# A block-placed copy of the values: GpSimd products with a mask column in the place of DMA copies

## What is computed

```python
xa = layer_norm(x)
w, k, v, r, g = projections(xa, shifted(xa))      # w is a decay between 0 and 1
def step(s, rkvw):                                # one token, per head, s is 16 x 16
    a = k_t[..., :, None] * v_t[..., None, :]
    out = einsum('bhi,bhij->bhj', r_t, u * a + s)
    s = a + w_t[..., :, None] * s
    return s, out
out = group_norm(scan(step, s0, (r, k, v, w))) * silu(g)
x1 = x + out @ Wo.T
x2 = x1 + sigmoid(xr2 @ Wfr.T) * (relu(xk2 @ Wfk.T) ** 2 @ Wfv.T)
```

## Time and profile before

| | |
|---|---|
| median of 3 runs | 3357.83 us (3356.09 to 3358.71) |
| the profiled execution | 3359.69 us, its span 3358.0 us |
| TensorE matmuls, weight loads | busy 95%, 71% |
| VectorE, ScalarE, GpSimd | busy 78%, 56%, 7% |
| mean granted TensorE clock | 0.987 of full speed |
| L1921 issues on GpSimd | 192, 528 ns mean |
| L489 issues on SP | 192, 64 KB each, median 1.9 us to landing |

### The profile page before, as it was taken

How to read it: one execution, slowest core, us unless ns; L and a number is a source line. 1 busy time by engine, 2 the same in 40 slices (tenths; PEclk the granted TensorE clock), 3 DMA queues, 4 the chain that set the end, 5 groups by cost and what they waited for, 6 DMA issues and landing times.

```text
span 3358.0 us, 77396 instructions
## 1 busy us (share of the span) xinstructions
PE 3205.9 (95%) x33056; PEld 2390.2 (71%) x33056; DVE 2628.4 (78%) x3721; ACT 1884.6 (56%) x3113; POOL 226.0 (7%) x457
## 2 busy tenths in 40 slices
PE   6889999999999999999999999998999999998998
PEld 4667777777777777777777777776566666665666
DVE  2888888989888888888888898987447567566566
ACT  2556555565565555555555555554346656556555
POOL 0000000000000000000000000000101010010110
PEclk8889999999999999999999999999999999999999
DMA  3113322333333223333332233324324234133221
GB/s 117 60 70 114 114 101 98 121 139 106 110 114 114 103 97 123 121 117 114 114 114 101 98 119 125 103 106 159 107 57 116 51 75 111 32 89 103 62 68 48
DMA packets 91924, 336.82 MB, mean 100 GB/s; under 512 B 16704, under 2 KB 37824, under 8 KB 65600
## 3 DMA queue, kind: packets, MB, share of 16 engines
q0 software_dynamic: 39936, 234.91, 21.6%
q1 hardware_dynamic: 51216, 93.68, 8.7%
q10 hardware_dynamic: 432, 3.28, 0.2%
HBM read 252.11 MB, written 16.78 MB: 80 GB/s over the span
## 4 chain that ended last, share of the span: by engine, by line
PE 73%; DVE 21%; ACT 3%; issue 1%; DMA 1%; SPq 0%; DVEq 0%; ACTq 0%
PE psum L729 31%; DVE rw L1647 6%; PE psum L738 6%; PE psum L904 5%; PE psum L922 3%; DVE rw L1630 3%; PE psum L874 3%; PE psum L864 3%; PE psum L779 3%; PE psum L894 3%; DVE rw L1529 2%; DVE psum L1737 2%; PE psum L879 2%; DVE rw L1535 2%; PE psum L682 2%; PE psum L803 1%
## 5 line engine op out<-in xcount | busy, mean ns | idle before, releaser
L729 PE MATMUL psum<-rw 128*128 128x256 f32 x6144 | 1412.7, 385 | 10.3 <-DVE rw L1535 4.9
L729 PEld LDWEIGHTS psum<-rw 128*128 128x128 f32 x6144 | 1150.8, 191 | 214.1 <-issue 42.6
L1647 DVE TENSOR_TENSOR rw<-rw 128x2048 f32<-128x2048 f32 x192 | 432.8, 2286 | 33.4 <-PE psum L803 30.3
L1737 DVE CUSTOM_DVE_ANT_0 psum<-psum,mem 128x1024 f32<-128x1024 f32 x256 | 313.4, 1224 | 81.1 <-PE psum L894 80.9
L1286 ACT ACTIVATE rest<-psum,mem 128x1024 f32<-128x1024 f32 x256 | 284.9, 1113 | 80.1 <-DVE mem L1737 78.4
L1195 ACT ACTIVATE rw<-psum 128x512 f32<-128x512 f32 x192 | 199.3, 1150 | 128.8 <-PE psum L779 128.8
L904 PE MATMUL psum<-ident,rest 128*128 128x128 f32 x2048 | 269.4, 275 | 0.2 <-ACT mem L1279 0.2
L904 PEld LDWEIGHTS psum<-ident,rest 128*128 128x128 f32 x2048 | 235.0, 141 | 38.5 <-issue 13.1
L1529 DVE SCALAR_TENSOR_TENSOR rw<-psum,rw 128x256 f32<-128x256 f32 x480 | 196.1, 475 | 83.4 <-PE psum L695 43.5
L1921 POOL DMA_DIRECT2D rw<-big_dram x192 | 101.2, 528 | 2309.6 <-PE psum L729 2275.7
L894 PE MATMUL psum<-side 128*128 128x512 f32 x512 | 211.8, 495 | 23.0 <-ACT rest L1286 20.7
(11 more groups left out here) (153 smaller groups left out, 4421.3 us busy)
## 6 DMA issues: line engine op xcount, KB each, us to landing
rw<-big_dram POOLq DMA_DIRECT2D x192, 1024.0 KB, 5.2
side<-mem POOLq DMA_DIRECT2D x256, 128.0 KB, 4.3
rw<-xs_dram SPq DMA_DIRECT2D x32, 512.0 KB, 3.5
side<-mem SPq DMA_DIRECT2D x256, 64.0 KB, 2.1
rw<-rw SPq DMA_DIRECT2D x192, 64.0 KB, 1.9
xs_dram<-rw SPq DMA_DIRECT2D x24, 512.0 KB, 5.3
rw<-x_dram SPq DMA_DIRECT2D x16, 512.0 KB, 3.6
mem<-xs_dram SPq DMA_DIRECT2D x16, 512.0 KB, 4.4
```

The lines of the kernel that those rows point to most:

```text
L729: last = mm(t[:, o * TC:(o + 1) * TC], big[:, k, P * m:P * m + P], src[:, k, 0:TC], start=k == 0, stop=k == KT - 1, skip_group_check=True)
L1647: state_dve.inc(tt(s_bd[:, half, :, :].rearrange("p c (h j) -> p c h j", h=4), own, place, ALU.mult), it, f"b{k}{half}")
L1737: maxima.inc(nc.vector.tensor_tensor_reduce(t, t, mbias.rearrange("p (a s) -> p a s", a=2), 1.0, 3.4e38, ALU.add, ALU.min, accum_out=mx[:, ...
```

## The change

`v_m` is filled by GpSimd: for each unit and pair four `tensor_scalar` products, each over all 128 partitions and 512 columns, of `v_t` with one column of a mask `place`, which is 1 on the partitions of chunk c and 0 elsewhere. VectorE makes the mask at the start. The clear of `v_m` and SP's copies go. GpSimd's weight loads, before one loop over the list, are now written in TensorE's order, and the products stand between them. The waits of the products are those that the copies had. The first weight loads now stand behind the wait for the constants.

```diff
+        place = sb("place", [P, 4])
...
-        vm_loaded = sem("vm_loaded")
+        chunks = Steps(sem("chunks"), ["m0", "m1"])
...
             for s in range(ITS + 2):
                 e, c, b, n = s - 2, s - 1, s, s + 1
-                if b < ITS:
-                    load_vm(b, 0)
                 if 1 <= n < ITS - 1:
                     load_xl(n + 1)
-                if b < ITS:
-                    load_vm(b, 1)
...
                 if n == 0:
-                    pe.wait_ge(vm_loaded, 16 * 4 * (2 * it + pair + 1))
+                    pe.wait_ge(chunks.sem, chunks.at(it, f"m{pair}"))
...
-            cleared(part_of("v_m"))
...
-            dve.wait_ge(const_ready, 9)
+            nc.vector.tensor_reduce(place[:], ident[:].rearrange("p (m c) -> p c m", c=4), AX_X, ALU.add).then_inc(const_ready, 1)
+            dve.wait_ge(const_ready, 10)
...
-            for turn, (it, which) in enumerate(weights):
-                if turn >= NSLOT:
-                    old_it, old = weights[turn - NSLOT]
-                    tiles, name = last_tile[old]
-                    pool.wait_ge(tiles.full, tiles.full_at(old_it, name))
+            pool.wait_ge(const_ready, CONSTS)
+
+            def fetch(turn):
+                it, which = weights[turn]
                 nc.gpsimd.dma_start(part_of(f"slot{turn % NSLOT}"), a["big"][layer_of(it), which]).then_inc(slot_loaded[turn % NSLOT], 16)
 
+            def after(it, which):
+                tiles, name = last_tile[which]
+                pool.wait_ge(tiles.full, tiles.full_at(it, name))
+                if turn_of[it, which] + NSLOT < len(weights):
+                    fetch(turn_of[it, which] + NSLOT)
+
+            def by_chunk(it, pair):
+                if pair == 0:
+                    pool.wait_ge(*b_ring.empty_at(it, "VT1"))
+                    if it:
+                        pool.wait_ge(b_ring.full, b_ring.full_at(it - 1, "U13"))
+                else:
+                    pool.wait_ge(b_ring.full, b_ring.full_at(it, "U03"))
+                for c in range(4):
+                    last = nc.gpsimd.tensor_scalar(v_m[:, :, c, :], v_t[:, :, 256 * pair:256 * pair + 256], place[:, c:c + 1], None, ALU.mult)
+                chunks.inc(last, it, f"m{pair}")
+
+            for turn in range(NSLOT):
+                fetch(turn)
+            for s in range(-1, ITS + 2):
+                e, c, b, n = s - 2, s - 1, s, s + 1
+                has_e, has_c, has_b, has_n = 0 <= e < ITS, 0 <= c < ITS, 0 <= b < ITS, n < ITS
+                if has_e:
+                    after(e, WFR)
+                if has_b:
+                    by_chunk(b, 0)
+                if has_c:
+                    after(c, WO)
+                if has_e:
+                    after(e, WFK)
+                if has_b:
+                    by_chunk(b, 1)
+                if has_e:
+                    after(e, WFV)
+                if has_n:
+                    after(n, WV)
+                    after(n, WK)
+                    after(n, WR)
+                    after(n, WG)
```

More of the change, by code:

```diff
@@ L133 @@
 OUT_PE = ["b00", "b01", "b10", "b20", "b21", "b30"]
-CONSTS = 10
+CONSTS = 11
 def laid_out():
@@ L477, in store_x @@
                 sp.dma_start(a["xs"][half_of(it), batch_of(it)], x1_flat[it % 2]).then_inc(x_stored, 16)
[L479 to L489, removed]
             def load_context(b):
@@ L1162, in spread_queries @@
                 if it == 0:
-                    act.wait_ge(zeroed, 3)
+                    act.wait_ge(zeroed, 2)
                 else:
```

## The result

The changed kernel takes 3624.46 us (median of 4 runs, 3622.98 to 3633.61), beside 3358.27 for the kernel before (4 runs). The ratio is 1.0786, with a 95% interval of 1.0765 to 1.0807: 7.9% slower. The profiled execution took 3624.39 us, its span is 3622.3, 264.3 more than before. The prediction said 3363, with a range of 3352 to 3400.

The account below looks back on a forecast made before the run. The prediction took TensorE, almost never idle in the units between 220 and 900 us, as the bound. 5.5 + 3.2 - 3.8 = +4.9 us on the profiled 3359.7 gave 3364.6, so 3363 for the median, range 3352 to 3400.

Parts of the forecast that it names:

- What bounds the kernel, and where the products must fit: Units at 220 to 900 us: TensorE busy 676.8 of 680.0; room 11.1 us for pair 0, 8.1 for pair 1.
- the first rival: Pair 1's last products let in late around VectorE's run: 3374 to 3384, some 3420 with the clock down; chance 0.30.
- The price of one product: GpSimd's 128x512 product: 0.65 us, between 0.52 and 1.08; four make 2.6 us.
- Does it disturb VectorE?: Both pairs: the products' full 2.6 us charged as a delay of VectorE, absorbed by its own slack.
- The wait of L662 for L1484: Pair 0: TensorE waits 0.25 us for late VectorE in each of 22 units, 5.5 us.
- Both signs: Prediction wrong if a product costs over 0.8 us, or the clock falls below 1.00 between 220 and 2300 us.
- The other edits: SP's issues, GpSimd's weight-load order, later first loads, v_m's clear, mask column: together nothing.
- What is gained: Unit of 1462 us: the 2.08 us copy wait and L729's slower matmuls behind it go, 3.8 us together.
- The 2.08 us at 1462: TensorE's wait for SP's copies in a middle unit, 2.08 us, expected gone.
- The sum: Whole kernel: 5.5 for pair 0, 3.2 for units 0 and 1, less 3.8 gained: +4.9 us.

Follow-up runs that it names:

- e4: Changed kernel with 12 memsets of 128x512 in place of each four products: 3375.70 us, ratio 1.0039 to the kernel before.
- e7: Changed kernel with e1's edit, and VectorE waiting for pair 1's products ahead of its run: 3509.39 us, ratio 1.0439 to the kernel before.
- e3: Changed kernel with products over 256 of the 512 columns, the other half of v_m left zero: 3402.17 us, ratio 1.0119 to the kernel before.
- e1: Changed kernel with GpSimd waiting for a weight's last reader only where a load follows: 3609.05 us, ratio 1.0732 to the kernel before.
- e8: Kernel before, with GpSimd waiting for the constants ahead of its first three weight loads: ratio 0.9989 to the kernel before.
- e9: Kernel before with weight loads in TensorE's order and e1's edit, SP's DMA copies kept: ratio 0.9982 to the kernel before.

## Why the prediction was wrong

**What bounds the kernel, and where the products must fit.** Right. TensorE had 11.1 and 8.1 us of room, the wait beyond that came through in full, and, as the first rival had it, the clock's fall came on top.

**The price of one product.** Wrong by a factor of 2.4: 0.65 us, with ends of 0.52 and 1.08, against 1.55 for 512 columns and 0.91 for 256 (2.5 ns a column and 0.27 fixed). Both neighbours that I used, a memset's slope and an affine_select of 128 columns with all above 0.10 us by column, lie below it, so the range had no upper end. By itself this mis-sizing costs nothing from unit 2 on: 6.2 us are still less than 8.1, and in e4 and e7 TensorE waits for GpSimd only in units 0 and 1 (7.6 and 8.3 us in all).

**Does it disturb VectorE?** This is the step that failed. "I charge the full 2.6 us as a delay of VectorE" put the loss on the wrong engine. VectorE keeps its times, but for 0.1 to 0.4 us (the L1469 group 2.02 in place of 1.66); GpSimd waits, in pair 1 through a whole run of VectorE's work. The wait of L662 for L1484, 0.25 us a unit, didn't appear. The first rival had the mechanism, chance 0.30: products let in late, around VectorE's run, and a clock that falls behind the wait. It had 3420 as its end because it took 0.65 us a product and thought that VectorE was open after the second L1535. With 1.55 us only one product fits in ahead of that run, and the fourth meets the next run, the block products; the wait is 8.3 us and not 1.2. Price and shutting out multiply: with products of 0.91 us, e3, the same mechanism costs 0.9 us a unit. Both signs that the prediction named for being wrong were seen, a product above 0.8 us and a clock below 1.00 in the units (0.95).

The Trainium skill, SBUF — State Buffer, section Who interferes with whom, states that a VectorE instruction with two SBUF inputs contends with a GpSimd instruction that reads SBUF and not with one that only writes it. The runs agree (e7 and e3 for the one, e4 for the other). The same section of the Trainium skill calls the shared ports an exclusive lock and says that the order of issue decides who blocks. Of this the runs show one side: a product that started second waited, and one under way wasn't stopped. The other side isn't seen: VectorE operations that started beside a product under way lost 0.1 to 0.4 us, not the rest of the product, and a waiting product stood through three of VectorE's instructions and not one.

The Trainium skill, GPSIMD Engine Reference, section Elementwise — side-by-side cycle accounting, gives 769 ns measured for 512 elements; as an estimate of one product it is half of the 1.55 us that the trace shows.

**The other edits: "nothing".** Wrong twice. I followed the weight loads unit by unit but not to the end of the list, where the next work on GpSimd's queue is the attention's: +18 us (e1). And I priced the later first loads by when a weight is read and not by what they stood in front of: the small start loads, on which VectorE waited until 14.1 us: -4 to -5 us (e8).

**What is gained.** The 2.08 us at 1462 us went, but the reason given isn't needed for it: they are gone in e9 too, which keeps SP's copies and has the weight loads in another order. In the time the gain can't be told apart from the rest: the intervals of e8 and e9 overlap.

**The sum.** 22 x 0.25 + 3.2 - 3.8 = 4.9 us became some 250 us in the units (23 waits, 196.1 us in all, where the copies had cost 8.6, and about 61 us of slower matmuls, 3266.7 us of TensorE's time in e1 beside 3205.9), +18 at the attention's start and -4 to -5 at the start of the kernel.

## What to carry to other kernels

Before work that reads memory goes to GpSimd, list what VectorE runs beside it: the time to reckon with is GpSimd's own, and for each of its instructions that starts beside a VectorE operation on two memory operands the rest of that back-to-back run. That is an upper bound, since some products here were let in before the end of a run. Where an upper bound of a price comes from a small neighbour, leave it open, and ask what happens if it is double: here a second run of VectorE came into reach. When a queue's order is rewritten, follow it to its last entry and to the first entry of what comes next, and ask at the start what each moved transfer stood in front of.

## What was not expected of the hardware

A GpSimd TENSOR_SCALAR of 128x512 float32 takes 1.552 us at least, one of 128x256 0.912, a memset of 128x512 0.518; ScalarE takes 0.707 for the same product and VectorE 0.480. A product beside VectorE's operations took up to 8.14 us. The clock's price for a TensorE wait of 8.3 us was 2.2 us in the stretch behind it. With three 1 MB loads issued at 2.4 us, a 0.5 KB load issued at 3.1 us took 11.0 us to land; with the three issued at 3.8 us (e8) it took 2.9, and VectorE, which had waited for it until 14.1 us, started at 8.7. When a waiting product is let in between two VectorE operations stays open: between the scan and the mixture behind it that happened in e3 and not in most units of the changed kernel.
